# A graph layer whose TensorE program is written out instead of looped

## The reference

```
agg  = segment_sum(x[src], dst)        # over the edges of each node, its own loop among them
mean = agg / max(deg, 1)
h    = mean @ W_l + b + x @ W_r
out  = layernorm(x + h * sigmoid(h))   # over the 512 features, eps 1e-5
```

## Time and profile before

| | |
|---|---|
| median of 3 executions | 1673.95 us (1671.81 to 1675.46) |
| the profiled execution | 1673.7 us, of which the span from first to last instruction is 1671.9 us |
| PE busy | 96% of the span, granted clock 0.99 of full speed |
| DVE busy | 85% |
| ACT, POOL busy | 62%, 61% |
| DMA engines | 256 GB/s over the span, reads and writes together |

### The profile page before, as it was taken

How to read it: one execution, slowest core, us unless ns; L and a number is a source line. 1 busy time by engine, 2 the same in 40 slices (tenths; PEclk the granted TensorE clock), 3 DMA queues, 4 the chain that set the end, 5 groups by cost and what they waited for, 6 DMA issues and landing times.

```text
span 1671.9 us, 30356 instructions
## 1 busy us (share of the span) xinstructions
PE 1602.2 (96%) x7886; PEld 1315.8 (79%) x7886; DVE 1413.4 (85%) x2174; ACT 1035.4 (62%) x1433; POOL 1015.3 (61%) x1307
## 2 busy tenths in 40 slices
PE   7998899999999999999999999999999999999995
PEld 5887677777778788888878888887888888888884
DVE  7888899989995888888888888888888888888886
ACT  4443333333334677777767767777777776777775
POOL 6445555555553666666666666666666666666664
PEclk9999999999999999999999999999999999999998
DMA  5445688878884666656666666665666666666664
GB/s 182 148 163 175 190 255 248 254 233 249 254 242 141 197 203 209 227 195 223 202 200 227 197 220 209 211 223 191 211 216 205 226 199 220 208 202 224 199 221 158
DMA packets 204144, 349.26 MB, mean 209 GB/s; under 512 B 37020, under 2 KB 51126, under 8 KB 204117
## 3 DMA queue, kind: packets, MB, share of 16 engines
q1 hardware_dynamic: 156135, 274.22, 49.1%
q0 software_dynamic: 46944, 74.22, 16.6%
q10 hardware_dynamic: 1038, 0.50, 0.1%
HBM read 288.78 MB, written 139.67 MB: 256 GB/s over the span
## 4 chain that ended last, share of the span: by engine, by line
issue 28%; PE 27%; POOL 19%; DVE 12%; ACT 9%; POOLq 2%; DVEq 1%; DMA 1%; SPq 0%; ACTq 0%
PE pH L498 23%; POOL cor L399 6%; ACT O L742 4%; DVE Z L1011 4%; DVE stats L1026 3%; POOL rstd L470 3%; POOL light_cor L399 3%; PE pT L566 2%; POOL l_var_eps L450 2%; ACT cor L696 2%; POOL var_eps L467 2%; ACT light_o L759 2%; DVE l_stats L1053 2%; POOL l_rstd L452 1%; PE pT L507 1%
## 5 line engine op out<-in xcount | busy, mean ns | idle before, releaser
L498 PE MATMUL pH<-ws_hi,x_hi 128*128 128x512 f32 x1564 | 631.5, 404 | 21.2 <-issue 14.6
L498 PE MATMUL pH<-ws_hi,x_lo 128*128 128x512 f32 x1564 | 613.8, 392 | 0.0
L498 PE MATMUL pH<-ws_lo,x_hi 128*128 128x512 f32 x1564 | 611.7, 391 | 0.0
L399 POOL DMA_INDIRECT cor<-correction_rows,node_now x347 | 370.6, 1068 | 215.5 <-POOL node_now L431 148.5
L498 PEld LDWEIGHTS pH<-ws_hi,x_hi 128*128 128x128 f32 x1564 | 295.3, 189 | 85.6 <-issue 30.8
L750 ACT ACTIVATE Z<-Z 128x1024 f32<-128x1024 f32 x174 | 184.2, 1059 | 284.7 <-DVE Z L1011 174.2
L498 PEld LDWEIGHTS pH<-ws_hi,x_lo 128*128 128x128 f32 x1564 | 294.9, 189 | 64.5
L498 PEld LDWEIGHTS pH<-ws_lo,x_hi 128*128 128x128 f32 x1564 | 295.7, 189 | 55.3
L742 ACT ACTIVATE O<-Z,shift,rstd 128x512 f32<-128x512 f32 x347 | 261.4, 801 | 3.7 <-DVE shift L1037 3.7
L1011 DVE TENSOR_TENSOR Z<-pH,cor 128x1024 f32<-128x1024 f32 x174 | 212.0, 1218 | 35.7 <-issue 23.8
L1026 DVE BATCH_NORM_STATS2 stats<-Z 128x6 f32<-128x512 f32 x347 | 221.5, 680 | 0.0
(11 more groups left out here) (134 smaller groups left out, 1834.1 us busy)
## 6 DMA issues: line engine op xcount, KB each, us to landing
X<-in_x SPq DMA_DIRECT2D x173, 512.0 KB
out<-O SPq DMA_DIRECT2D x173, 512.0 KB
correction_rows<-c_out SPq DMA_DIRECT2D x98, 256.0 KB
light_x<-in_x SPq DMA_DIRECT2D x66, 256.0 KB, 2.6
light_h<-early_product SPq DMA_DIRECT2D x44, 256.0 KB
out<-light_o SPq DMA_DIRECT2D x44, 256.0 KB
join_row<-joined SPq DMA_DIRECT2D x98, 64.0 KB
light_h<-in_x SPq DMA_DIRECT2D x22, 256.0 KB, 2.7
```

The source lines that it names most:

```text
L399: g.indirect_dma_start(out=out_, out_offset=None, in_=table, in_offset=bass.IndirectOffsetOnAxis(ap=idx, axis=0), bounds_check=bound, oob_ ...
L498: last = mm(ps, a[:, k], w[:, k], start=(n == 0), stop=(n == len(terms) - 1))
```

## The change

The four loops of TensorE's program are written out; its instructions with work in them, their order and their waits' meaning stay. The other engines keep their loops.

```
-            looped(pe, 2, MERGE_ROUND, early_tile)
+            peeled(8, 4 * MERGE_ROUND, early_tile)
...
-            looped(pe, MERGE_ROUND, FIND_ROUND, early_tile)
+            peeled(4 * MERGE_ROUND, 4 * FIND_ROUND, early_tile)
...
-            steps(pe, ET, edge_tile)
+            peeled(0, ET, edge_tile)
...
-            steps(pe, NP, node_pair)
+            peeled(0, NP, node_pair)
```

## The result

| | median, us | range | executions |
|---|---|---|---|
| before | 1673.09 | 1671.65 to 1675.64 | 12 |
| changed | 1669.95 | 1668.47 to 1672.57 | 12 |

The ratio is 0.998, with a 95% interval of 0.9972 to 0.9989: 3.1 us less, clear of noise, and 0.35 us from the forecast of 1670.3. That it came so near is partly luck: executions of one kernel spread over 4 us, and the forecast stood on a median of 3 executions, 0.9 us above the one of 12.

What follows compares the result with a forecast made beforehand. The prediction took a TensorE-VectorE ring to bound the edge stage and a VectorE-ScalarE-GpSimd ring the node stage; 3.4 + 0.2 + 0 + 0 = 3.6 us off 1673.7 gave 1670.1, plus 0.25 for the median 1670.3 us, range 1662 to 1675.

Steps and rivals of the forecast that it cites:

- Edge turns: Edge stage: TensorE's tile at its loop's turn starts earlier once written out, 0.16 us a round, 21 rounds, 3.4 us.
- the other late one: Edge stage: the late mid-round tile of the four, 3.50 us, forecast to stay so.
- c_out's 0.2 us: Edge stage: the extra delay of VectorE's c_out after TensorE's matmuls, said to belong to VectorE's loop, which stays.
- Node loop: Node stage: TensorE's 40 loop turns give 0 us, covered by VectorE's ring; at most 24.8 us without that cover.
- TensorE catching up with VectorE: Node stage: TensorE, once held up, ran 25.36 us a round against VectorE's 25.98, gaining 0.6 us a round.
- Registers in mid-round: Edge stage: constants in place of registers give TensorE nothing in mid-round, at most 2.3 us.
- Early stage: Early stage, six rounds: 0.2 us gained for all turns, between 0 and 1.0.
- Longer code: TensorE's instruction queue grows from 11 to some 62 packets, 1.0 MB, at a price of 0.
- The ring of the node stage: Node stage: VectorE, ScalarE and GpSimd in a ring make the round 25.98 us, and TensorE waits out the difference.
- The first rival: TensorE's gaps are all its own: 1661 us for the edge part (10%), 1636 with the node stage too (2% for both).
- TensorE's floor: TensorE's own pace without waits: 3.24 us an edge tile, 25.36 us a node round.

Runs made afterwards that it cites:

- e4: Against the kernel before, VectorE's edge loop written out and TensorE's not: 1659.76 us, ratio 0.9917.
- e2: Against the kernel before, only TensorE's node-stage loop written out: 1672.34 us, ratio 0.9998.
- e10: Against the changed kernel, TensorE does the first transpose of every node pair twice: 1668.54 us, ratio 0.9975 to the kernel before.
- e9: Against the changed kernel, every engine's edge and node loops written out, SyncE's too: 1624.32 us, ratio 0.9689 to the kernel before.
- e8: Against the changed kernel, the node loops of VectorE, ScalarE and GpSimd written out, SyncE's kept: 1671.56 us, ratio 0.9974 to the kernel before.
- e12: Against the changed kernel, the node loops of all four other engines written out, their edge loops kept: median 1672.75 us.

## Why the prediction was right

- **Edge turns, 0.16 us x 21 = 3.4.** Right in size: rounds fell from 13.56 to 13.40, and this loop alone gave 3.5 us. Half a miss in the form: I had put the whole cut on the tile at the turn (3.58 to 3.42, the other late one left at 3.50). Most rounds have three late tiles of four, 3.42, 3.29 and 3.45. The odd tile behind the one at the turn started 0.20 us after its s_lo before; now it starts 0.10 after it, so it waits for VectorE as well, and the same sum spreads over three.
- **c_out's 0.2 us are VectorE's and stay.** Right, and shown by writing that loop out (e4).
- **Node loop, nothing.** Right: e2 and e10. The reading that decided it was TensorE catching up with VectorE in the earlier trace rows, over nearer three rounds than the four that it names (no gap from 1157 to 1234 us). Had the profile's word "issue" been taken as TensorE's own delay, the forecast would have been 1636. One premise was wrong: the gap is not at the turn of TensorE's loop, but one pair behind it.
- **Registers in mid-round, nothing.** Consistent with 13.40; not measured alone.
- **Early stage, 0.2.** Not resolved by any run.
- **Longer code, nothing.** 62 packets forecast, 64 read. e2 has most of them and is no slower, and with all loops written out (e9) TensorE runs node rounds of 25.36 us one after the other without a gap. The prediction goes too far where it says that the trace disagrees with the Trainium skill (Runtime: NRT & Kernel Launch, Instruction fetch mechanics): the 128 matmuls and weight loads of an edge round are half a packet of 256 instructions, so by that rule, too, its turn would mostly stay within two pages and need no fetch. The 11 packets show that the 61 turns did not each cost a fetch, not that the rule is wrong.
- **The ring of the node stage** was right as a bound on TensorE and incomplete as a mechanism. I took 25.98 us for a property of the ring's work and loops; it moved between 25.87 and 26.07 with edits elsewhere, and a step of GpSimd that takes 1.1 us longer beside VectorE's residual add goes with 1.0 us of it. With few such steps the ring is no longer than TensorE's 25.36.
- **The first rival** was wrong for this change, but its numbers return as soon as the other engines are written out too: 3.24 a tile and 25.36 a round. TensorE's floor had been read rightly; the slack above it belonged to others.

## What to carry to other kernels

A gap called issue that comes once a round isn't yet the turn of that engine's loop: see where the loop's branch stands in the engine's own instruction queue, look for what ended 0.1 us before the gap's end on the engines that feed it, and for a stretch in which the engine caught up. When several engines form a ring, a loop is worth writing out first on the one whose looped waits are in the ring (here VectorE's edge loop: 13 us, 8.4 of them in its own rounds), and an engine that seems busy 96% of the time can have room: double a small piece of its work and see if that is paid.

## What the runs showed of the hardware

**A turn's own instructions.** The trace of before lists them for the queue of TensorE's weight loads, per turn of the edge loop (ns: least, median, most):

```profile
L214 PEldq FUSED_REGOPS  x21: 44/44/55, 205.6 to 480.1; - x21
L214 PEldq ALU_OP  x21: 32/32/32, 218.9 to 493.3; - x21
L214 PEldq COMPARE_BRANCH  x21: 76/208/227, 219.0 to 493.4; - x21
```

Together 0.28 us, of which 0.14 to 0.16 reach the matmuls. The median branch takes 208 ns, twice the 108 ns that the prediction quotes from the Trainium skill (Advanced Engine Details and Errata, Control Flow Timing); on VectorE it takes 56 ns and on ScalarE 45.

**VectorE's c_out starts 0.2 us later in a loop.** Where it waits for TensorE (the even tiles), c_out starts some 0.24 us after the last matmul's end in the loop and 0.03 to 0.05 in written-out code, in mid-round as at a turn. It is not a price of every wait in a loop: s_lo, which waits for ScalarE's s_hi, starts 0.03 to 0.04 us after it in the looped and in the written-out kernels alike (medians). What sets c_out apart was not looked into. TensorE's looped waits showed nothing like it in mid-round (0.10 us after s_lo, as in written-out code).

**A step of GpSimd beside VectorE's two-operand add takes 1.1 us longer.** In e8 the gather that starts at 910.67 ends at 912.74 instead of about 911.67, and VectorE's add beside it ends at 911.86. The Trainium skill (SBUF — State Buffer, SBUF: two separate sides) says that GpSimd and VectorE share a pair of ports as an exclusive lock, which a VectorE instruction with two SBUF inputs takes against a GpSimd instruction that reads SBUF. The rows agree in kind: the delay of 1.07 us is about what was left of the add. So do the counts. Of 122 rstd in e8 (600 to 1400 us) the 30 that start within 0.03 us of the add take 1.8 us; all others take 0.72 or 0.73, among them those that started 0.11 us or more ahead of it. For the gathers some 0.01 us decides: in e12, 15 of the 18 that start 0.01 or 0.02 us after the add take 1.0 us, and all 12 that start later within it are long, the less so the later (2.06 us at 0.03, 1.74 at 0.34). No run tested it by moving either instruction.
